# Decoder layer on one core: the seam between attention and experts re-ordered, the last output projection cut into pieces

## What is computed

```
x = layernorm(x + self_attention(x))                 # 16 heads of 16, rotary
x = layernorm(x + cross_attention(x, ctx))           # 16 heads of 64
x = layernorm(x + moe(x) + swiglu(x, sw1, sw2, sw3)) # 8 experts, top 2 by x @ gate_w
swiglu(x, w1, w2, w3) = (silu(x @ w1) * (x @ w2)) @ w3   # hidden width 512
```

## Time and profile before

| | |
|---|---|
| median of 3 executions | 724.55 us (719.53 to 729.85) |
| the profiled execution | 718.07 us |
| its span in the profile | 716.2 us |
| instructions | 14309 |
| mean granted clock of TensorE | 0.922 of full |
| end of attention's last DVE instruction, start of the expert block | 535.05, 535.55 us |
| first tile's low part on DVE | 589.73 us |
| bytes moved | 57.34 MB, 80 GB/s |

### The profile page before, as it was taken

The page is one execution under the profiler, slowest core; times in us unless marked ns, Lnnn a source line. Parts: engine busy times, 40 slices in busy tenths (PEclk is TensorE's granted clock), DMA queues, the critical chain, the costliest instruction groups (busy, mean ns, idle before and its releaser), DMA issues. The chain is left out here.

```text
span 716.2 us, 14309 instructions
## 1 busy us (share of the span) xinstructions
PE 587.8 (82%) x4746; PEld 454.8 (63%) x4746; DVE 477.2 (67%) x903; ACT 408.4 (57%) x995; POOL 267.2 (37%) x297
## 2 busy tenths in 40 slices
PE   4743867899999999999999999998759778899980
PEld 3533656777777777777777777777556464566650
DVE  3895347867877877877877877866737686633332
ACT  2444337577577677677677677664427646643431
POOL 3462014353343343343343344334421741333332
PEclk9865589999999999999999999999866999999995
DMA  8625110210210210210210210311207576333324
GB/s 227 223 99 178 30 47 30 61 42 31 61 41 29 57 43 28 55 45 27 54 47 27 53 48 21 116 53 31 90 33 260 167 246 227 61 61 57 56 30 110
DMA packets 58069, 57.34 MB, mean 80 GB/s; under 512 B 17266, under 2 KB 47218, under 8 KB 58034
## 3 DMA queue, kind: packets, MB, share of 16 engines
q1 hardware_dynamic: 53650, 50.89, 22.9%
q0 software_dynamic: 4384, 5.99, 4.9%
HBM read 46.74 MB, written 10.13 MB: 79 GB/s over the span
## 5 line engine op out<-in xcount | busy, mean ns | idle before, releaser
L653 POOL TENSOR_TENSOR c_rcp<-c_sum,neg_one 112x2 f32<-112x2 f32 x64 | 44.5, 696 | 199.9 <-ACT probs L796 199.9
L657 POOL TENSOR_TENSOR probs<-probs,c_rcp 112x750 f32<-112x750 f32 x64 | 91.9, 1435 | 5.0
L796 ACT ACTIVATE probs<-ps_s,c_neg 112x375 f32<-112x375 f32 x128 | 72.6, 580 | 22.2 <-DVE c_neg L1028 21.7
L688 ACT ACTIVATE kt_hi<-ps_o 128x376 fp32r<-128x376 f32 x64 | 31.8, 497 | 67.6 <-PE ps_o L151 67.6
L1023 DVE SCALAR_TENSOR_TENSOR v_lo<-ps_vx,v_scale,v_hi 125x512 f16<-125x512 f32 x48 | 35.9, 749 | 42.6 <-ACT v_hi L788 42.2
L1661 POOL DMA_INDIRECT moe_sum<-gsh_hi,xs_in x21 | 33.7, 1607 | 80.4 <-ACT gsh_hi L1712 65.1
L1032 DVE SCALAR_TENSOR_TENSOR cpt_lo<-ps_t,cpt_hi 125x672 f16<-125x672 f32 x64 | 54.4, 849 | 12.4 <-ACT cpt_hi L803 12.4
L1028 DVE TENSOR_REDUCE c_neg<-ps_s 112x2 f32<-112x750 f32 x64 | 59.4, 929 | 1.4 <-PE ps_s L151 1.4
L1974 PE MATMUL ps_h<-w_ex,xst_hi 128*128 (+1 forms) x168 | 58.0, 387 | 2.5 <-DVE xst_lo L1751 2.4
L1350 PE MATMUL ps_t<-ident,probs 112*128 112x112 f32 x384 | 49.3, 266 | 8.8 <-DVE cpt_lo L1032 8.5
L149 PE MATMUL ps_o<-ctxt_hi,w_k_lo 128*128 128x376 f32 x128 | 48.8, 382 | 8.7 <-DVE oct_lo L916 7.6
(11 more groups left out here) (313 smaller groups left out, 1799.9 us busy)
## 6 DMA issues: line engine op xcount, KB each, us to landing
chunk<-in_L_ffn_ew_dram SPq DMA_DIRECT2D x24, 512.0 KB, 3.5
spare<-in_L_ffn_ew_dram SPq DMA_DIRECT2D x18, 512.0 KB, 6.1
store<-in_L_ffn_ew_dram SPq DMA_DIRECT2D x6, 512.0 KB, 5.8
ctx_all<-in_ctx_dram SPq DMA_DIRECT2D x2, 1500.0 KB
ctx_raw<-in_ctx_dram SPq DMA_DIRECT2D x8, 375.0 KB
moe_in<-chunk SPq DMA_DIRECT2D x1, 2709.0 KB, 13.5
plain_raw<-in_L_xattn_w_kv_dram SPq DMA_DIRECT2D x2, 1024.0 KB, 15.1
xs_in<-moe_in SPq DMA_DIRECT2D x15, 129.0 KB, 2.0
```

Of the source, the lines that this page charges most:

```text
L653: pool.tensor_tensor(c_rcp[:, s % 2, :], c_sum[:, s % 2, :], neg_one[:, :], ALU.pow).then_inc(sg["c_rcp_ready"], 1)
L657: pool.tensor_tensor(p, p, r, ALU.mult).then_inc(sg["p_normed"], 1)
L796: act.activation(probs[:, s % 2, h, 0:SK], ps_s[0:N, h, 0:SK], ACT.Exp, bias=c_neg[:, s % 2, h:h + 1], accum_out=c_sum[:, s % 2, h:h + 1]) ...
```

## The change

In attention:
- The last entry's `cross_out` runs in pieces: pairs 0 to 2 in step 6, pair 3 in step 7, pair 4 behind the loop ahead of the last `p_transpose`, pair 5 behind `pv` of pair 6, pairs 6 and 7 at the end.
- Behind the loop PE transposes x2 of entries 0 to 3 (8 transposes into ps_a), ACT and DVE split them. ACT's order becomes x2t's high parts, `cpt_hi(7)`, `o_hi(6)`, gw's high part, `o_hi(7)`.
- `scales` moves here in three parts (`weight_maxima`, `weight_powers`, `weight_scales`) between DVE's last five instructions of attention, with its two PE transposes (now through ps_s) between the pieces of `cross_out`; gw's two parts too.

In the expert block:
- Only entries 4 to 7 are transposed and split; the logits of entries 0 to 3 wait for nothing of it.
- `convert(0, 2)` stands behind `top_two`; `top_weights` and `slots` stand ahead of `gate(0)`; `rank_tokens` stands behind the first half of unit 0.
- Two memsets of POOL go (the mask v_mask gets two more columns in its place).

Buffers gw, x2t and the scales are allocated for the whole program; in preparation two temporaries share memory with others.

```diff
@@ ACT, behind the loop
+            for i in range(KD):
+                act.wait_ge(sg["x2t_full"], i + 1)
+                act.activation(x2t[0][:, i, 0:HALF], ps_a[:, i, 0:HALF], ACT.Copy, scale=X_SCALE).then_inc(sg["x2t_hi"], 1)
+            cpt_hi(B - 1, 7)
             o_hi(B - 1, 6)
-            cpt_hi(B - 1, 7)
+            act.wait_ge(sg["scaling"], 10)
+            act.activation(gw[0][:, :, :], gw_raw[:, :, :], ACT.Copy, scale=s_cols[:, 3:4]).then_inc(sg["gw_hi"], 1)
             o_hi(B - 1, 7)
@@ DVE, behind the loop
             cpt_lo(B - 1, 6)
+            weight_maxima()
+            for i in range(KD):
+                dve.wait_ge(sg["x2t_hi"], i + 1)
+                dve.scalar_tensor_tensor(x2t[1][:, i, 0:HALF], ps_a[:, i, 0:HALF], X_SCALE, x2t[0][:, i, 0:HALF],
+                                         op0=ALU.mult, op1=ALU.subtract).then_inc(sg["x2t_lo"], 1)
+            weight_powers()
             o_lo(B - 1, 6)
             cpt_lo(B - 1, 7)
+            weight_scales()
+            dve.wait_ge(sg["gw_hi"], 1)
+            dve.scalar_tensor_tensor(gw[1]...
             o_lo(B - 1, 7)
@@ PE, in the loop and behind it
+                    if not more and s >= 6:
+                        cross_out(b, range(0, 3) if s == 6 else range(3, 4))
...
+            pe.wait_ge(sg["x2_ready"], 4)
+            for i in range(KD):
+                for j in range(4):
+                    last = pe.transpose(ps_a[:, i, j * N:(j + 1) * N], x2_all[0:N, j, i * P:(i + 1) * P], ident[0:N, 0:N])
+                last.then_inc(sg["x2t_full"], 1)
+            cross_out(B - 1, range(4, 5))
             p_transpose(B - 1, 7)
             pv(B - 1, 6, PAIRS * B)
-            cross_out(B - 1, range(0, 6))
+            pe.wait_ge(sg["scaling"], 2)
+            pe.transpose(ps_s[0:4, 0, 0:P], m_cols[:, :], ident[:, :]).then_inc(sg["scale_full"], 1)
+            cross_out(B - 1, range(5, 6))
+            pe.wait_ge(sg["scaling"], 5)
+            pe.transpose(ps_s[:, 1, 0:4], m_row[:, :].to_broadcast([4, P]), ident[0:4, 0:4]).then_inc(sg["scale_full"], 1)
             pv(B - 1, 7, PAIRS * B)
             cross_out(B - 1, range(6, PAIRS))
@@ expert block, DVE
-            scales()
-            for i in range(4):
+            for i in range(KD):
                 x2t_lo(i)
...
-            for i in range(3):
+            for i in range(2):
                 convert(0, i)
             top_two()
+            convert(0, 2)
             for u in range(UNITS):
-                gate(u, HALF)
                 if u == 0:
                     top_weights()
                     slots()
+                gate(u, HALF)
@@ expert block, PE
-            pe.wait_ge(sg["x2t_lo"], 5)
             for b in range(B):
+                if b == 4:
+                    pe.wait_ge(sg["x2t_lo"], KD)
...
+                    if u == 0 and i == 0:
+                        rank_tokens()
...
-                if u == 0:
-                    rank_tokens()
```

More of the change, by code:

```diff
@@ L169, in product_over_width, with preparation_block @@
     return last
[L172 removed]
+def preparation_block(nc, sg, A, ident, consts, weights, qk_rot, v_all, v_cols, spare):
     w_k, w_v, w_q, w_o, w_proj = weights
@@ L455, in expert_weights, with attention_block @@
     return tuple(A[n][e] for n in ("ew1", "ew2", "ew3"))
-def attention_block(nc, sg, A, x2_all, ident, consts, weights, qk_rot, v_all, raw, ffn_sg, w_max, gw_raw, xs, v_cols):
+def attention_block(nc, sg, A, x2_all, ident, consts, weights, qk_rot, v_all, raw, ffn_sg, w_max, gw_raw, xs, v_cols, gw, x2t,
+                    scales):
+    m_cols, m_row, p_cols, s_cols, unscale, c_gate, c_y = (scales[n] for n in ("m_cols", "m_row", "p_cols", "s_cols",
+                                                                              "unscale", "c_gate", "c_y"))
     w_k, w_v, w_q, w_o, w_proj = weights
@@ L1187, in iteration, with weight_maxima @@
                         chunk_max(3 * b + s - PAIRS + LATE)
+            def weight_maxima():
+                dve.wait_ge(sg["chunk_max"], CHUNKS)
+                dve.tensor_reduce(m_cols[:, 0:3], w_max[:, :].rearrange("p (j i) -> p i j", i=3), X, ALU.max)\
+                    .then_inc(sg["scaling"], 1)
+                dve.wait_ge(ffn_sg["gw_loaded"], 16)
+                dve.tensor_reduce(m_cols[:, 3:4], gw_raw[:, :, :].rearrange("p k e -> p (k e)"), X, ALU.max,
+                                  apply_absolute_value=True).then_inc(sg["scaling"], 1)
@@ new lines, in weight_powers @@
+            def weight_powers():
+                dve.wait_ge(sg["scale_full"], 1)
+                dve.reduce_max(m_row[:, :], ps_s[0:4, 0, 0:P], X).then_inc(sg["scaling"], 1)
+                dve.wait_ge(sg["scaling"], 3)
+                dve.tensor_scalar(m_row[:, :], m_row[:, :], 2.0 ** -100, None, ALU.max).then_inc(sg["scaling"], 1)
+                dve.wait_ge(sg["scaling"], 4)
+                dve.tensor_tensor(m_row[:, :].bitcast(I32), m_row[:, :].bitcast(I32), v_mask[0:4, 0:1].bitcast(I32),
+                                  ALU.bitwise_and).then_inc(sg["scaling"], 1)
@@ L1669, in _ @@
         def _(act):
-            for i in range(4):
[L1671 to L1675, removed]
+            for k in range(KD):
+                act.wait_ge(sg["x2t_full"], k + 1)
+                act.activation(x2t[0][:, k, half(1)], ps_h[:, k, 0:HALF], ACT.Copy, scale=X_SCALE).then_inc(sg["x2t_hi"], 1)
             def convert(j, i):
@@ L1787, in x2t_lo @@
[L1787 to L1790, removed]
+            def x2t_lo(k):
+                dve.wait_ge(sg["x2t_hi"], k + 1)
+                lo(x2t[1][:, k, half(1)], ps_h[:, k, 0:HALF], X_SCALE, x2t[0][:, k, half(1)]).then_inc(sg["x2t_lo"], 1)
             def top_two():
@@ L2126, in decoder_layer @@
         gw_raw = outer.enter_context(nc.sbuf_tensor("gw_raw", [P, KD, EXP], F32))
+        gw = half_pair(nc, outer, "gw", [P, KD, EXP])
+        x2t = half_pair(nc, outer, "x2t", [P, KD, TOK])
+        scales = {n: outer.enter_context(nc.sbuf_tensor(n, shape, F32)) for n, shape in
+                  (("m_cols", [P, 4]), ("m_row", [4, 1]), ("p_cols", [P, 4]), ("s_cols", [P, 4]), ("unscale", [P, 4]),
+                   ("c_gate", [P, 1]), ("c_y", [P, 1]))}
         xs = nc.dram_tensor("moe_in", (SLOTS, XW), F32).ap()
@@ L2138, in decoder_layer @@
             v_cols = ctx.enter_context(nc.sbuf_tensor("v_cols", [P, 3], F32))
-            preparation_block(nc, signals[0], A, ident, consts, weights, qk_rot, v_all, v_cols)
+            preparation_block(nc, signals[0], A, ident, consts, weights, qk_rot, v_all, v_cols, x2t[0])
             signals[0].clear()
-            attention_block(nc, signals[1], A, x2_all, ident, consts, weights, qk_rot, v_all, raw, signals[2], w_max, gw_raw, xs, v_cols)
+            attention_block(nc, signals[1], A, x2_all, ident, consts, weights, qk_rot, v_all, raw, signals[2], w_max, gw_raw, xs, v_cols, gw, x2t,
+                            scales)
         signals[0].release()
-        ffn_block(nc, signals[2], A, x2_all, ident, store, w_max, gw_raw, xs, out)
+        ffn_block(nc, signals[2], A, x2_all, ident, store, gw, x2t, scales, xs, out)
 def rope_table():
```

91 lines of the change are left out of this document (28 added, 63 removed).

## The result

| | before | after |
|---|---|---|
| median of 20 executions each | 719.55 us (715.88 to 729.85) | 714.54 us (711.44 to 722.57) |
| ratio, with its 95% interval | | 0.9931 (0.9911 to 0.9951) |
| the profiled execution, its span | 718.07, 716.2 us | 714.09, 712.3 us |
| mean granted clock of TensorE | 0.922 | 0.931 |
| attention's last transposes start | 524.08 us | 524.71 us |

The change takes 5.0 us off the medians and 4.0 us off the profiled executions; both are under 1%. The three executions of before that the prediction had were a high draw: their median of 724.55 us is 5.0 us over that of twenty.

What follows compares the result with a forecast made beforehand. TensorE, busy 82% of the span, was taken as the bound, with winnable idle time at the blocks' seam. Gains of 1.7 and 2.25 us made 4.0: 724.55 - 4.0 = 720.5 us, range 713.5 to 727.5 (8 in 10).

Steps and rivals of the forecast that it cites:

- the likeliest case: Whole kernel, the forecast itself: a gain of 3 to 5.5 us, 719 to 721.5 us, chance 0.50.
- Nothing in the loop: Attention steps 6 and 7: moved projection pieces gain 0, as the reload loop sets the period; at most 0.5 us lost.
- later than 524.08: Attention's end: the last transposes starting after 524.08 us was named as a sign of being wrong.
- Behind the loop: Attention's end: 0.7 us from a shorter last chain plus 1.0 from the high clock, 1.7 us gained.
- four hand-overs: Attention's last pair: ACT and DVE alternate on gate weights and outputs, 0.3 to 0.4 us each, until about 530.3.
- The logits: Expert block's start: logits end 6.1 us after the block starts instead of 10.15, so 4.05 us earlier.
- From the logits to `gate(1)`: Expert block: 10.7 us instead of 8.9, so the new order costs 1.8; net block gain 2.25 us.
- What lies behind: From `gate(1)` to the first tile: same list, so everything just shifts by 4.0 us.
- Slack of the scatter: Ahead of the tiles: slots ready almost 7 us earlier, at 547.75, so scattered rows do not hold the tiles.
- The clock stays low through the shared units: Rival, expert block: units at 4.5 us each, 1 us later than before, 725.5 us; chance 0.10.
- The clock helps more: Rival, expert block: high clock kept through transposes, logits and unit 0; gain about 7 us, 717.5; chance 0.12.
- Part of it is held up: Rival, seam: last chain pushed back or an assumed slack path binds; gain 0 to 2.5 us, 722 to 724.5; chance 0.25.

Runs made afterwards that it cites:

- e8: Kernel after with 16 unread transposes filling TensorE's wait behind the loop, ahead of the eight real ones; 714.3 us, ratio 0.9934.
- e1: Kernel after with the expert block's whole old order (converts ahead of top_two, gate(0) ahead of weights and slots, ranks behind unit 0); 714.54 us, ratio 0.9915.
- e2: Kernel before with only the expert block's new order; 721.76 us, ratio 1.0022.
- e11: Kernel after, its own order kept, with 16 and 12 unread transposes filling both idle TensorE stretches of the seam; 714.31 us, ratio 0.9908.
- e5: Kernel after run again unchanged, on another chip; 716.36 us, ratio 0.9926.
- e6: Kernel after with gate(0) back ahead of weights and slots and ranks behind unit 0, convert(0, 2) left behind top_two; 716.17 us, ratio 0.9937.
- e9: e6 with both idle TensorE stretches of the seam filled by 16 and 12 unread transposes; 712.49 us, ratio 0.9901.
- e10: e1 with both idle TensorE stretches of the seam filled by 16 and 12 unread transposes; 711.79 us, ratio 0.9877.
- e13: The kernel of e9, unchanged, run a second time; 713.25 us, ratio 0.9888.
- e3: Kernel before with only the last output projection spread over steps 6, 7 and the gaps behind the loop; 721.65 us, ratio 0.9995.
- e12: e3 with 24 unread transposes in TensorE's idle stretch behind the loop; 715.71 us, ratio 0.9943.

## Why the prediction was right, and where not

The forecast of a gain of 4.0 us stood against 4.0 in the profiled executions and 5.0 in the medians, so the likeliest case came true by its gain (3 to 5.5), though not by its time (719 to 721.5); the absolute 720.5 stood 6.0 over the measured median. Of these 5.0 are the base: the working hung the difference on the median of three (724.55) although it knew that the profiled execution, 718.07, was 6.5 us under it. The median of twenty lies 1.5 over the profiled one. The range held because it allowed for such a draw, and with little to spare: 714.54 lies 1.0 us above its lower end.

Point by point:

- **Nothing in the loop: right in kind.** `chunk_max` of step 7 still waits for its DMA, 0.54 us at 522.58, so the reload loop sets the period of the last steps. That the last transposes came 0.63 us later is in the range in which T moves by itself; "later than 524.08" had been named as a sign of being wrong, and it was a bad sign to choose, since a single execution can't hold it.
- **Behind the loop: 1.04 us for 1.7.** Two terms were off. The clock was expected high for the last transposes and `pv(6)`, "as TensorE works nearly without a gap": the eight transposes run at the high clock and take 0.98 us, not 1.7, so the gap stayed at 2.48 us, and in this execution the clock fell at 525. Estimating at the low clock a filling meant to keep the clock high was the slip. Against e8 the low clock cost 1.6 us here; in e1, where the eight did run low (1.76 us) and the gap was 0.43 us, T to M is 5.85 us. Four profiles of these lists, unfilled, lie between 5.85 and 7.82, two of before's at 7.40 and 8.47, so one pair could not have tested this term, and its 1.04 us is not more than luck would give. And the "four hand-overs" ahead of `o_lo(7)` don't exist: the split of the gate's weights (529.34 to 529.9) lies beside `pv(7)`, and `o_hi(7)` waits 0.20 us for TensorE alone.
- **The logits: right.** The block starts at 535.14 (x2_norm's end and 0.5 us), the logits end at 541.33: 6.2 us for 6.1.
- **From the logits to `gate(1)`: right.** `gate(0)` 7.75 us behind them for 7.8, `gate(1)` 2.88 later for 2.9, X to G a gain of 2.23 for 2.25. That the new order costs there was right too: 1.8 by the sum, 1.5 and 2.4 by e1 and e2 (the 2.4 with a low clock in it).
- **What lies behind: more than a shift.** 1.09 us from G to F weren't in the sum. In the kernel before DVE waits at the shared expert's end for TensorE, which was at the low clock from 581 to 584.5; in the kernel after the same instructions, of the same kinds, follow without a wait. First before, then after:

```profile
582.63 0.48 DVE L1889 SCALAR_TENSOR_TENSOR ffn_res<-ps_out,c_y,x_all 112x256 f32<-112x256 f32 x1 [0.67 <-PE ps_out L1974]
...
584.96 0.48 DVE L1889 SCALAR_TENSOR_TENSOR ffn_res<-ps_g,c_y,x_all 112x256 f32<-112x256 f32 x1 [0.66 <-PE ps_g L1974]
```
```profile
579.64 0.48 DVE L1904 SCALAR_TENSOR_TENSOR ffn_res<-ps_out,c_y,x_all 112x256 f32<-112x256 f32 x1
...
581.23 0.48 DVE L1904 SCALAR_TENSOR_TENSOR ffn_res<-ps_g,c_y,x_all 112x256 f32<-112x256 f32 x1
```
  The kernel after has 34.0 in both its profiles, but e8 and e11, with the same list from G on, have 35.25 and 35.06: whether the change keeps this gain depends on where the clock stands, and the sum can't count on it. With the 0.2 us behind F it covered the 0.66 us missing behind the loop and the 0.63 us by which T came later: that the profiled difference came out at 4.0 is luck. From T on, which the sum was about, the gain is 4.5 us, and 5.1 in e5.
- **Slack of the scatter: right.** It begins at 549.46 (548 forecast), and POOL's first read waits 1.92 us for the last of it, long before the first tile:

```profile
573.92 3.36 POOL L1702 DMA_DIRECT2D xs_in<-moe_in x6 [1.92 <-DMA moe_in<-w_ex,slot]
```
  The first tile is held by DVE's own list, so scattering earlier bought nothing, and the price paid for it at `gate(0)` was for nothing: e1, e6, e9, e10 and e13 go back on it.

The rivals. *The clock stays low through the shared units* was wrong: it rose at 549, 1.4 us earlier than before, and fell only at 562.7, behind a wait of TensorE of 4.20 us. The Trainium skill's rule ("TensorE: Matmul & The Clock Gate", section "A second HAM failure mode: psum-queue depth-cycling") is that short idle times between groups of matmuls make the clock swing. The trace shows no swing between 549 and 562.7, but TensorE has no idle time there before the one of 4.20 us, so it doesn't test the rule. The prediction had read from it that every unit could run at 4.5 us; that did not happen. As a warning the rival is not far off: e3's execution held the low clock until 559, and its X to G is 1.2 us longer. *The clock helps more* didn't happen in the change, and where TensorE did enter the block at the high clock (e9, e13) it did not keep it: the transposes gave 0.77 us, the 0.8 of its working, but unit 0 still took 4.1 to 4.3 us, so X to G gained 0.73 us over e6 where the working had 3. *Part of it is held up* happened in the attention block and was made good elsewhere.

## What to carry to other kernels

Before shortening a seam, ask what TensorE does in it: here work put into its idle stretches went with 1.7 to 4.4 us in four pairs of profiles and next to nothing in two, and e12 came near the change's ratio that way. Before naming the clock in one pair of profiles as the effect of an edit, look at how it moves between executions of the same lists: T to M did so by 2 us. Size work that should hold the clock with durations at the clock it should hold. And put forward work that something waits for: the slots had slack on their side, `gate(0)` had none, and moving them past each other cost 1.5 to 2.4 us from X to G for nothing.

## What the runs showed of the hardware

- The clock fell 0.4 us behind the end of a TensorE wait of 2.48 us (after, 525) and not behind one of 0.97 us with the filling ahead of it (e8). But it also fell with TensorE busy all through the half microseconds around (0.50 of 0.50): at 524.9 in e6, with 1.51 us, ended at 523.71, as the last wait before it, and at 524.4 in e5.
- In e13 it fell between 537 and 538 although TensorE was busy all through (1.00 in the windows of 536 and 537), with the 48 logit matmuls of 8 columns; their pitch was 0.05 us before and 0.09 us after the fall.
- In e12 it rose from 0.50 to 1.00 between 523.5 and 524, during 24 transposes without a gap.
- The same TensorE list lost the clock 4.3 us behind T in one execution and 10.1 to 10.9 us behind it in three others; entries of the loop take 53.9 or 55.4 us. The two profiles of the kernel after differ by 3.1 us ahead of T and by 0.6 us behind it.
